# Normalising x of the next chunk on VectorE instead of GpSimd, in slot 2 of every chunk

## The reference, cut to what matters

```python
xn = _layernorm(x)                      # (x - mean) / sqrt(var + 1e-5), per row of 128
x + state_space(xn) + moe_ffn(xn)

# state_space: a recurrence over time for each of 128 features and 16 states
dt = soft_clamp(softplus(xn @ Wdt.T + bdt), 0.001, 0.1, 0.5)
dA = exp(soft_clamp(dt[..., None] * A, -8, 8, 0.5));  B = xn @ WB.T;  C = xn @ WC.T
h = dA_t * h + dt_t * B_t * xn_t;   y_t = sum_n(h * C_t) + Dp * xn_t

# moe_ffn: 64 experts (8 chosen for each token by group-limited top-k) and a shared one
combine[t, e] = 2.5 * score / sum(chosen scores)
routed = sum_e combine[:, e] * (relu(xn @ up_w[e])**2 @ down_w[e])
shared = relu(xn @ shared_up_w)**2 @ shared_down_w
```

## Time and profile before

| what | value |
|---|---|
| median of three runs | 572.5 us (572.01 to 573.7) |
| the profiled execution | 574.56 us, of which the span from first to last instruction is 572.8 us |
| PE busy | 508.6 us (89%) |
| DVE busy | 496.0 us (87%) |
| ACT busy | 470.4 us (82%) |
| POOL busy | 469.3 us (82%) |
| granted TensorE clock | 0.998 of full speed |
| DMA | 149.32 MB, mean 261 GB/s |

### The profile page before, as it was taken

How to read it: one execution, slowest core, us unless ns; L and a number is a source line. 1 busy time by engine, 2 the same in 40 slices (tenths; PEclk the granted TensorE clock), 3 DMA queues, 4 the chain that set the end, 5 groups by cost and what they waited for, 6 DMA issues and landing times.

```text
span 572.8 us, 7918 instructions
## 1 busy us (share of the span) xinstructions
PE 508.6 (89%) x1666; PEld 278.0 (49%) x1666; DVE 496.0 (87%) x1158; ACT 470.4 (82%) x922; POOL 469.3 (82%) x430
## 2 busy tenths in 40 slices
PE   2158899998898988999899998999989998999996
PEld 1034445554454545565455544555445554555552
DVE  3657899899988899899998899888998899979984
ACT  2768798799886998888986998879988889988872
POOL 2389898897888979897988978889897979968762
PEclk9999999999999999999999999999999999999999
DMA  8956865887869877987678877697769877699951
GB/s 200 326 166 229 277 258 197 318 291 259 247 191 348 276 261 232 347 271 262 247 239 307 304 264 248 197 364 264 272 216 321 300 249 246 219 318 353 317 189 37
DMA packets 65649, 149.32 MB, mean 261 GB/s; under 512 B 14048, under 2 KB 31040, under 8 KB 65600
## 3 DMA queue, kind: packets, MB, share of 16 engines
q1 hardware_dynamic: 63728, 147.07, 76.3%
q10 hardware_dynamic: 1872, 1.75, 0.9%
HBM read 143.03 MB, written 5.77 MB: 260 GB/s over the span
## 4 chain that ended last, share of the span: by engine, by line
POOL 28%; issue 22%; DVE 18%; PE 14%; ACT 8%; DMA 8%; SPq 1%; POOLq 1%; DVEq 0%; ACTq 0%
POOL yacc L546 10%; DMA bc_rows<-bc_dram 7%; PE DN L1088 7%; POOL bc_rows L537 6%; DVE DC L944 4%; DVE relu L885 4%; POOL xn L444 3%; DVE g L831 3%; DVE bc_rows L897 3%; PE U L1038 2%; PE U L1039 2%; PE U L1040 2%; ACT act L715 2%; POOL rstd L438 1%; POOL rest L527 1%
## 5 line engine op out<-in xcount | busy, mean ns | idle before, releaser
L1088 PE MATMUL DN<-act,down 128*128 128x512 f32 x512 | 261.9, 593 | 1.9 <-ACT act L715 1.9
L715 ACT ACTIVATE act<-relu 128x512 f32<-128x512 f32 x272 | 169.5, 623 | 44.6 <-DVE relu L885 38.3
L885 DVE SCALAR_TENSOR_TENSOR relu<-U,gate_rows 128x512 f32<-128x512 f32 x256 | 173.6, 678 | 34.0 <-PE U L1040 17.8
L546 POOL TENSOR_TENSOR yacc<-yacc,bc_rows 128x512 f32<-128x512 f32 x120 | 154.5, 1287 | 44.9 <-DVE bc_rows L897 44.9
L1038 PE MATMUL U<-x_hi,up_hi 128*128 128x512 f32 x256 | 163.4, 638 | 23.5 <-DVE relu L885 22.5
L537 POOL TENSOR_TENSOR bc_rows<-dtx_all,bc_rows 128x512 f32<-128x512 f32 x128 | 164.4, 1285 | 20.2 <-DMA bc_rows<-bc_dram 20.2
L944 DVE TENSOR_TENSOR_SCAN DC<-DC,carry,bc_rows 128x512 f32<-128x512 f32 x96 | 122.7, 1278 | 0.0
L1088 PEld LDWEIGHTS DN<-act,down 128*128 128x128 f32 x512 | 95.3, 188 | 28.7 <-ACT act L715 6.6
L1038 PEld LDWEIGHTS U<-x_hi,up_hi 128*128 128x128 f32 x256 | 48.2, 188 | 113.7 <-DVE relu L885 70.1
L1039 PE MATMUL U<-x_lo,up_hi 128*128 128x512 f32 x256 | 101.2, 395 | 0.0
L1040 PE MATMUL U<-x_hi,up_lo 128*128 128x512 f32 x256 | 101.1, 395 | 0.0
(11 more groups left out here) (113 smaller groups left out, 501.5 us busy)
## 6 DMA issues: line engine op xcount, KB each, us to landing
bc_rows<-bc_dram SPq DMA_DIRECT2D x128, 512.0 KB, 6.0
gate_rows<-gate_dram SPq DMA_DIRECT2D x128, 512.0 KB, 4.8
xs<-in_L_attn_x SPq DMA_DIRECT2D x8, 256.0 KB, 5.6
down<-in_L_ffn_down_w SPq DMA_DIRECT2D x8, 256.0 KB, 4.9
xr<-in_L_attn_x SPq DMA_DIRECT2D x8, 256.0 KB, 5.6
rest_kept_dram<-rest SPq DMA_DIRECT2D x8, 256.0 KB, 4.3
out<-res SPq DMA_DIRECT2D x8, 256.0 KB, 4.5
dtx_all<-in_L_ffn_up_w SPq DMA_DIRECT2D x3, 512.0 KB, 5.6
```

The lines of the kernel that those rows point to most:

```text
L546: g.tensor_tensor(yacc[:, :], yacc[:, :], c_rows[:, (c * N + n) % BUFS, :], ALU.add).then_inc(yacc_done, 1)
L715: a.activation(act_at(c, slot), relu[:, slot % 2, :], ACT.Square).then_inc(sq_done, 1)
L885: v.scalar_tensor_tensor(out=relu[:, slot % 2, :], in0=U[slot % 2][:, :], scalar=0.0, in1=gate_rows[:, k // 2 % SBUFS, slot % 2, :], op0=A ...
L1088: mm(DN[:, :], w, act_at(c, slot), start=slot == 0, stop=slot == SLOTS - 1).then_inc(down_done, 1)
```

## The change

`xn` of the next chunk leaves GpSimd's slot 2. VectorE computes it in its own slot 2 of every chunk, behind the `ymul` of state 0 and ahead of the `mul` of slot 2, and waits there for `rstd_ready`. The step ahead of the loop (`pc == 0`) moves from slot 3 to slot 2 of the same engine.

```diff
-                if slot == 2 and pc:
-                    pool.wait_ge(rstd_ready, pc + 1)
-                    wait(pool, lgt_done, pc)
-                    alone(pool)
-                    for k in range(KB):
-                        i = g.tensor_scalar(xn[:, k, :], xs[:, k, :], mv[:, k, 0:1], rstd[:, k:k + 1],
-                                            ALU.subtract, ALU.mult)
-                    i.then_inc(xn_ready, 1)
...
-                if slot == 3 and pc == 0:
-                    dve.wait_ge(rstd_ready, 1)
+                if slot == 2:
+                    dve.wait_ge(rstd_ready, pc + 1)
+                    wait(dve, lgt_done, pc)
                     for k in range(KB):
                         i = v.tensor_scalar(xn[:, k, :], xs[:, k, :], mv[:, k, 0:1], rstd[:, k:k + 1],
                                             ALU.subtract, ALU.mult)
```

## The result

The changed kernel takes 582.05 us (median of four runs, 579.42 to 583.62) against 572.58: 1.0158 times the time before, 95% interval 1.0116 to 1.0200. The profiled execution takes 583.62 us, with a span of 581.8 where it was 572.8.

A forecast was written before the change was run, and what follows sets the result against it. It took the path from rstd through xn, transposes, x_hi and x_lo to the projections as the bound. 6 x 0.55 + 5 x 1.2 + 0 = 9.3 us on 572.5 gave 582 us, range 577 to 586.

The forecast's parts named there:

- The bound and the price one to one: At each chunk's start, the path from rstd to the projections bounds; lateness at the projections reaches the end in full.
- The wait (1): VectorE waits for rstd_ready in slot 2, idle 3.0 us in chunk 2, 1.1 to 3.0 us in the six chunks.
- The four and the stream behind (2, 3): Four xn 0.26 us apart on VectorE, then queued work: projections 7.2 us after rstd, not 6.65, +0.55 a chunk.
- The contention (4): VectorE's xn held by GpSimd's inject(c, 3): some 1.2 us in five of six chunks, bounds 0 and 4 x 1.25.
- Chunk 0 (5): In chunk 0 GpSimd's split delays the four xn; taken as 0, between -2.2 (not held) and +0.9 (held twice).
- A: VectorE's xn isn't held by GpSimd: +1.1 us, 573.6 us; chance 0.16.
- B: VectorE's lateness at x_lo goes through in full to the end: +15.3 us, 588 us; chance 0.19.
- C: rstd comes ahead of VectorE, so the wait and TensorE's idle time go: -5.9 us, 566.6 us; chance 0.07.
- D: Later chunk starts are made up by shorter waits on transfers: within 0.3%, 572.5 us; chance 0.06.

The follow-up runs named there:

- the wait alone: Kernel before, with VectorE waiting for rstd in slot 2 of every chunk while xn stays on GpSimd: 572.48 us against 572.61, ratio 0.9997.
- the kernel without the hold: Changed kernel, with GpSimd waiting for xn_ready behind rstd so that nothing of GpSimd runs beside xn: 574.24 us, ratio 1.0018.

## Why the prediction was right, point by point

**The bound and the price one to one.** It holds in chunks 1 to 6, within 0.4 us each. It doesn't hold in chunk 0, as the run with the wait alone shows. Keeping TensorE from its idle time ahead of the transposes made the kernel faster, as that reading says.

**The wait (1).** Foreseen at 1.1 to 3.0 us a chunk, found at 0.24 to 3.52. In five of the six chunks `rstd` came 0.2 to 0.9 us earlier against the chunk's first `mul` than before, in chunk 2 0.6 later. I had it fixed; it moves with the row transfers. Over the six chunks that is some 2.5 us in the changed kernel's favour, not in my sum. But the kernel with the wait alone, whose GpSimd does the same work as before, has `rstd` earlier by the same 2.5 us in all. So that this comes of the change isn't shown; one profiled execution differs from another by as much. That the wait itself costs nothing while something stands beside it was shown by the wait alone.

**The four and the stream behind (2, 3).** Foreseen 7.2 us from `rstd` to the projections, not held; found 7.03 in chunk 4 and 7.03 to 7.15 with GpSimd out of the way. The term is 0.4 to 0.5, not 0.55. The 0.26 us a piece holds; the estimate of 127 ns by the Trainium skill's page "VectorE: DVE Perf Modes", section on the TRN2 errata, does not.

**The contention (4).** The two rows of the kernel before from which I took it told the truth: the earlier trace rows. Held in five of six chunks, as predicted by the landing of one row, and not in chunk 4. It costs 0.95 us and not 1.2: the held instruction ends with GpSimd's, so its own 0.26 us is hidden in the hold. That it is most of the loss is shown by the runs in which GpSimd waits.

**Chunk 0 (5)** is where the sum was wrong: 0 foreseen, 1.77 found, outside my own bounds of -2.2 to +0.9. Two steps of it failed. The first is the one `inject` that I let come after the four: it gets in among them, behind the split, so that they take 4.34 us. The second is that TensorE's clock had no term. With TensorE kept busy the four are held as long (4.43 us), `x_lo` starts 9.04 us after `rstd` and not 9.99, where it waited 0.97 us for `x_hi`, the projections are 14.8 us after the first `mul` and not 17.3, and the chunk is 0.8 us longer than before: inside the bound of +0.9 that I gave for two holds. The other 1.0 us goes with the clock. Part of the lateness is made up where VectorE waits for GpSimd's `sfc` in slot 13, 1.15 us instead of 2.46.

**The clock** wasn't in the prediction: in chunks 0 and 2 TensorE stood for 5.0 and 3.04 us and came back at half its clock.

So the mechanism was right in its largest terms, and that the total of 9.3 us came so near to 9.5 is luck. In the two profiled executions, 9.0 us apart: 6 x 0.45 + 5 x 0.95 = 7.5 us for the terms foreseen at 9.3; 1.1 for chunk 2 at the lower clock; 2.5 less by earlier `rstd`s; 1.0 that chunks 1 to 6 lose behind the projections, for which no run shows a cause; and 1.8 for chunk 0. Terms that I hadn't foreseen made up for terms that I had priced too high.

**The rivals.** A, VectorE isn't held, falls by the length of `xn`; but its price was near what the kernel without the hold takes, 574.24 against 573.6. B, all the lateness goes through, falls: at `x_lo` chunk 6 lost 7.39 - 4.86 = 2.53 us after `rstd`, at its projections 1.48. C, faster as `rstd` is ahead: it doesn't come about by itself. Forced, with `rstd` ahead and `xn` on VectorE, it gives the time of before, 573.67 us, as C had no price for the hold; with `xn` left on GpSimd early `rstd` gives 3 us. D falls.

## What to carry to other kernels

A step moved to another engine should be put where what it waits for has already come: the same four instructions cost 9.5 us in slot 2 and nothing in slot 3. Before giving VectorE an instruction with both ends in SBUF, look at what GpSimd issues at that same moment; here the end of `rstd` let both go on at once, VectorE by its semaphore and GpSimd to its next instruction, and they collided in all chunks but chunk 4, and one more wait on GpSimd was cheaper than the collision. Idle time that a profile shows as new isn't a price until something behind it is late; adding the wait alone tests that for the cost of two lines. And a price measured in one chunk isn't that of all: 1.5 us of lateness at the projections cost nothing in chunk 0.

## What the runs showed of the hardware that I had not expected

Four short instructions of VectorE in a row aren't one for GpSimd: each that is ready gets in between two of them. None beside them 1.12 us, one 2.07, two 2.81, a split of 2.59 us and an `inject` 4.34. The Trainium skill's page "SBUF — State Buffer", section "Who interferes with whom", says that whoever issues first keeps the other out for a whole instruction. These numbers agree, instruction by instruction: with two beside them the first of the four took 1.06 us and the second 1.32, each to the end of one of GpSimd's.

TensorE came back from its long stands at half its clock. The changed kernel behind the stand of 5.00 us in chunk 0, then the kernel before in its chunk 0 and chunk 2 (length of the stretch; busy time and count of PE, PEld, DVE, ACT and POOL; granted clock, DMA share, GB/s):

```profile
44.00:48.00 4.00, 2.79 (x5) 1.72 (x6) 4.00 (x9) 2.42 (x5) 0.45 (x1) 0.50 0.49 199
48.00:52.00 4.00, 4.00 (x13) 2.79 (x12) 3.03 (x5) 2.34 (x6) 2.98 (x3) 0.68 0.69 254
52.00:56.00 4.00, 4.00 (x16) 2.51 (x15) 3.17 (x5) 3.98 (x9) 4.00 (x3) 1.00 0.41 141
```
```profile
36.00:52.00 16.00, 11.37 (x38) 6.55 (x37) 11.66 (x16) 11.30 (x24) 15.73 (x15) 1.00 0.73 256
184.00:188.00 4.00, 4.00 (x15) 2.51 (x15) 3.87 (x6) 3.86 (x11) 4.00 (x4) 1.00 0.80 289
```

A granted clock of 0.50 is 1.2 GHz and 1.00 is 2.4; it was at 2.4 through both stretches before the change, so the prediction had no term for it. The length of the one stand doesn't tell whether the clock falls. In its chunk 0 the kernel before kept 2.4 GHz behind a stand of 2.43 us; the kernel with the wait alone fell to 1.2 GHz by the end of a stand of 2.31 us, though its TensorE does the same work (its transposes, then 46 to 48 us: busy time and count of PE, granted clock, DMA share, GB/s):

```profile
45.97 1.12 PE L1046 MATMUL M<-ident,xn 128*128 128x128 f32 x4 [2.31 <-POOL xn L444]
...
46.00:48.00 2.00, 2.00 (x7) 0.50 0.50 199
```
